# Linear attention on one core: norms of the queries split in token quarters, their factors multiplied in among the last queries, and all low halves on VectorE

## The chip, the cores and the metric

The kernel runs on one core of one Trainium2 chip. The metric is the device time of one execution in microseconds (us); for a kernel it is the median of several runs.

## The reference, cut to what matters

The program is two transformer layers over x of shape (4, 512, 256). The change lies in the first block alone, linear attention with 16 query heads and 4 key/value heads of 128, followed by a residual and a layer norm:

```
q = x @ Wq.T + bq ; k = x @ Wk.T + bk ; v = x @ Wv.T + bv     # 16, 4, 4 heads of 128
sq, sk = elu(q) + 1, elu(k) + 1
kv    = einsum('bhsd,bhse->bhde', sk, v)                       # k, v repeated for 4 query heads
norm  = einsum('bhsd,bhd->bhs', sq, sk.sum(axis=2))
attn  = (sq @ kv) / (norm[..., None] + 1e-6)
x     = layernorm(x + concat_heads(attn) @ Wo.T)
```

The 3 blocks behind it (a gated low-rank update, softmax attention, experts) make up the second phase.

## The kernel before, in words

The engines run queues of their own, in program order, and wait on semaphores. Phase 1 is `layer0_attention`, phase 2 `update_attention_experts`. Phase 1 handles the 4 batches of 512 tokens one after the other; what follows is one batch. P is 128, T is 512. "Head n" is the n-th in `ORDER0`: head j of each of the 4 groups g, then j + 1.

1. Keys and values: TensorE, L274, 4 token tiles, 48 matmuls of 512 columns. Every product of this phase with weights is done in three passes (`split_passes`) with values split into a high and a low half of type fp32r.
2. Queries: `query(n)` on TensorE (L303) is six matmuls of 512 columns into one of three PSUM banks `bank_q`. ScalarE takes min and exp (L426, L428), VectorE makes `sq[n]` (L522). `query(n)` waits until VectorE has read the bank of `query(n-3)`.
3. Norms: `norm(j)` (L316) multiplies the `sq` of the four heads of one j by `ksel` (the key sums placed in columns), 4 matmuls of 512 columns, each in its own 32 rows of `bank_n`. Two j share a half. VectorE then adds an epsilon (`invert`, L538), takes the reciprocal in two pieces of 256 columns (`invert_tokens`, L544), ScalarE makes a high half (`factor_hi`, L419), VectorE the rest (`parts`, L549).
4. Maps: `output_map(p)` (L331) makes kv @ Wo for two heads; ScalarE and VectorE split it (`map_hi` L414, `map_lo` L527). There are 8 maps per batch, in 4 buffers.
5. Factors: `factor(n)` (L345) is one matmul of 512 columns that spreads the reciprocal norms of head n over 128 rows of a `bank_q` bank. VectorE multiplies it into `sq[n]` (L601, "scale"). ScalarE makes `s_hi` (L468). The low half `s_lo` is VectorE's for even n (`scaled_lo`, L533) and GpSimd's for odd n (L229). `s_hi` and `s_lo` have two buffers each, so `s_hi(n)` waits for `project(n-2)`.
6. Projections: `project(n)` (L361) is 12 matmuls of 256 columns (4 token tiles, 3 passes) that add up in `bank_y`; it waits for `s_hi(n)` and `s_lo(n)`.

TensorE's order for a batch is written out by hand: keys and values, queries 0 to 2, the kv state (L286) and the key sums (L290), queries 3 to 15 with maps 0 to 3 behind queries 4, 6, 14 and 15 and norms 0 to 2 behind queries 5, 9 and 13, then factor 0, factor 1, norm 3, and for n = 0 to 15: `factor(n+2)`, `project(n)`, with maps 4 to 7 behind projects 1, 3, 5 and 7. VectorE's order in the last part is, for each n: scale(n), and for odd n `scaled_lo(n-1)` behind it; the inversion of the second half stands behind scales 0 to 2, a `map_lo` behind scales 4, 6, 8 and 10, the split of the next batch's x (`split_x`, 1024 columns) behind scale 12.

Of the kernel before, what the change touches and what calls it, by code (L numbers as in the profile page):

```python
# [16 lines left out]
P = 128  # L17
# [9 lines left out]
ORDER0 = [(g, j) for j in range(J0) for g in range(G0)]  # L27

# [85 lines left out]
def layer0_attention(nc, a, kept):  # L114

    with ExitStack() as ctx:
# [18 lines left out]
        pick_raw, pick = sb("pick_raw", [H0]), sb("pick", [H0], F32R)  # L135
# [7 lines left out]
        ksel = sb("ksel", [G0, J0, 32])  # L143
# [3 lines left out]
        den, rn = sb("den", [T]), sb("rn", [T])  # L147
        rn_c, rn_parts = sb("rn_c", [T], F32R), sb("rn_parts", [2, T], F32R)
        m_hi, m_lo = sb("m_hi", [4, 2 * D], F32R), sb("m_lo", [4, 2 * D], F32R)
        s_hi, s_lo = sb("s_hi", [2, T], F32R), sb("s_lo", [2, T], F32R)  # L150
# [25 lines left out]
        s_lo_ready = [sem("s_lo_ready_even"), sem("s_lo_ready_odd")]  # L176
# [5 lines left out]
        PARTS_AT = 10  # L182
        MAP_AT = (4, 6, 14, 15)
# [10 lines left out]
        def _(sp):  # L194
# [12 lines left out]
            with sp.Fori(0, B - 1) as b:  # L207
                after = sp.snap(b + 1)
                sp.wait_ge(xT_hi_ready, after)
                sp.wait_ge(xT_lo_ready, after)  # L210
                sp.dma_start(xT[:, :, :], a["xT"][:, bass.ds(after, 1)].rearrange("p o k n -> p (o k) n")).then_inc(xT_in, 16)
# [9 lines left out]
        def _(pool):  # L221
# [3 lines left out]
            def scaled_lo(b, n):  # L225

                pool.wait_ge(s_hi_ready, H0 * b + n + 1)
                at_least(pool, s_lo_ready[1], H0 // 2 * b + n // 2)
                pool.tensor_tensor(s_lo[:, 1, :], sq[:, n, :], s_hi[:, 1, :].bitcast(F32), ALU.subtract).then_inc(s_lo_ready[1], 1)  # L229

            def keep(b):

                pool.wait_ge(res_ready, b + 1)
                pool.wait_ge(s_lo_ready[1], H0 // 2 * (b + 1))
                pool.tensor_copy(tiles(xs, b), res[:, :, :]).then_inc(res_kept, 1)
# [9 lines left out]
            def body(b, last):  # L245
                sum_keys(b)
                if last:
                    keep(b - 1)
                pool.wait_ge(sk_sum_step, (NT - 1) * (b + 1))
                for n in range(1, H0, 2):  # L250
                    if n == 1:
                        at_least(pool, res_kept, b)
                    scaled_lo(b, n)
# [7 lines left out]
        def _(pe):  # L261
# [30 lines left out]

            def query(b, n):
                g, j = ORDER0[n]
                hd = slice((J0 * g + j) * DH0, (J0 * g + j + 1) * DH0)
                if n < 3:
                    at_least(pe, scaled, H0 * b)
                else:
                    pe.wait_ge(sq_ready, H0 * b + n - 2)
                i = 0  # L300
                for k in range(KD):
                    for lhs, rhs in split_passes(wq_hi[:, k, hd], wq_lo[:, k, hd], xT_hi[:, k, :], xT_lo[:, k, :]):
                        mm = pe.matmul(bank_q[n % 3][:, :], lhs, rhs, start=i == 0, stop=i == 3 * KD - 1)  # L303
                        i += 1
                mm.then_inc(q_done, 1)

            def norm(b, j):
# [27 lines left out]
            def factor(b, n):  # L335
# [5 lines left out]
                if n < 3:  # L341
                    pe.wait_ge(sq_ready, H0 * b + H0 + n - 2)
                else:
                    pe.wait_ge(scaled, H0 * b + n - 2)
                pe.matmul(bank_q[(H0 + n) % 3][:, :], pick[:, h:h + 1].broadcast_to([P, P]), rn_parts[:, n // (H0 // 2), :],  # L345
                          start=True, stop=True).then_inc(bc_done, 1)

            def project(b, n):
# [3 lines left out]
                pe.wait_ge(s_lo_ready[n % 2], H0 // 2 * b + n // 2 + 1)  # L352
# [4 lines left out]
                for t in range(NT):  # L357
                    tok = slice(t * P, (t + 1) * P)
                    for i, (lhs, rhs) in enumerate(split_passes(s_hi[:, n % 2, tok], s_lo[:, n % 2, tok], m_hi[:, m, cols], m_lo[:, m, cols])):
# [9 lines left out]
            def body(b, first):  # L369
                pe.wait_ge(xT_hi_ready, b + 1)  # L370
                pe.wait_ge(xT_lo_ready, b + 1)
# [11 lines left out]
                for n in range(3, H0):  # L383
# [21 lines left out]
        def _(act):  # L405
            def split_x(b):
                act.wait_ge(xT_in, 16 * (b + 1))
                at_least(act, q_done, H0 * b)
                act.activation(xT_hi[:, :, :], xT[:, :, :], ACT.Copy).then_inc(xT_hi_ready, 1)
# [6 lines left out]
            def factor_hi(b, half_):  # L416
                act.wait_ge(rn_ready, 2 * (2 * b + half_ + 1))
# [3 lines left out]
            def query_exp(b, n):  # L421
# [4 lines left out]
                act.activation(eq[:, n % 3, :], bank_q[n % 3][:, :], ACT.Relu, bias=bq_neg[:, h:h + 1], scale=-1.0).then_inc(eq_capped, 1)  # L426
# [14 lines left out]
            def body(b, first, more):  # L441
# [15 lines left out]
                for n in range(3, H0):  # L457
                    query_exp(b, n)
                    if n in MAP_AT:
                        map_hi(b, MAP_AT.index(n))  # L460
                    if n == PARTS_AT + 3:
                        factor_hi(b, 0)
                for n in range(H0):
                    if n == 4:
                        factor_hi(b, 1)
                    act.wait_ge(scaled, H0 * b + n + 1)
                    at_least(act, y_done, H0 * b + max(0, n - 1))
                    act.activation(s_hi[:, n % 2, :], sq[:, n, :], ACT.Copy).then_inc(s_hi_ready, 1)  # L468
                    if n in (3, 5, 7, 9):
                        map_hi(b, 4 + (n - 3) // 2)  # L470
                    if n == 10 and more:
                        split_x(b + 1)

            split_weights(0)
            split_x(0)
# [6 lines left out]
        def _(dve):  # L482
            def split_x(b):
                dve.wait_ge(xT_hi_ready, b + 1)
                at_least(dve, q_done, H0 * b)
                dve.tensor_tensor(xT_lo[:, :, :], xT[:, :, :], xT_hi[:, :, :].bitcast(F32), ALU.subtract).then_inc(xT_lo_ready, 1)
# [30 lines left out]
            def query(b, n):  # L517
# [4 lines left out]
                dve.scalar_tensor_tensor(out=sq[:, n, :], in0=bank_q[n % 3][:, :], scalar=bq1[:, h:h + 1], in1=eq[:, n % 3, :],  # L522
# [6 lines left out]
            def scaled_lo(b, n):  # L529
# [3 lines left out]
                dve.tensor_tensor(s_lo[:, 0, :], sq[:, n, :], s_hi[:, 0, :].bitcast(F32), ALU.subtract).then_inc(s_lo_ready[0], 1)  # L533

            def invert(b, half_):

                dve.wait_ge(norm_done, 2 * b + half_ + 1)
                dve.tensor_scalar(den[:, :], bank_n[:, :], DEN_EPS, None, ALU.add).then_inc(den_ready, 1)  # L538

            def invert_tokens(b, half_, i):  # L540

                dve.wait_ge(den_ready, 2 * b + half_ + 1)
                tok = slice(i * T // 2, (i + 1) * T // 2)
                dve.reciprocal(rn[:, tok], den[:, tok]).then_inc(rn_ready, 1)  # L544
# [14 lines left out]
            def residual_stats(b):  # L559

                dve.wait_ge(res_ready, b + 1)
                for t in range(NT):
                    dve.bn_stats(bn[:, t, :], res[:, t, :]).then_inc(bn_ready, 1)
                dve.wait_ge(bn_ready, NT * (b + 1))
# [3 lines left out]
            def body(b, last, more):  # L568
# [6 lines left out]
                for i in range(2):  # L575
                    at_least(dve, s_lo_ready[i], H0 // 2 * b)
# [1278 lines left out]
```

## Time and profile before

| what | value |
|---|---|
| runs timed | 834.54, 835.08, 848.41 us; median 835.08 |
| profiled execution | 842.74 us |
| its span (first to last instruction) | 840.7 us |
| TensorE, weight loads | 723.7 us (86%), 486.0 us (58%) |
| VectorE, ScalarE, GpSimd | 528.6 (63%), 410.0 (49%), 106.4 (13%) |
| mean granted TensorE clock | 0.9 |

Phase 1 takes the first 361 us of the span or so, phase 2 the rest. In the profile PE is TensorE's matmuls, PEld its weight loads, DVE VectorE, ACT ScalarE, POOL GpSimd. The duration of a matmul includes its pipeline, so a chain of matmuls is read by the distance of their starts.

### The profile page before, as it was taken

The page shows a single profiled execution, that of the slowest core. Times are in us where ns is not written, and L with a number is a line of the kernel's source. Part 1 is how long each engine was busy: PE and PEld are TensorE (multiplying, and loading weights), DVE is VectorE, ACT ScalarE, POOL GpSimd, SP SyncE. Part 2 cuts the span into 40 slices and gives each one's busy share as a digit, 9 for nine tenths or more (in the row PEclk, how much of TensorE's full clock was granted, in tenths as well). Part 3 has the DMA queues.
Part 4 walks back from the last instruction along what each step waited for, and adds up shares of the span by engine and source line. Part 5 has one row for each costly group of instructions (what it writes and reads, how often), then busy time and mean ns, then how long its engine had stood idle before and what let it go on. Part 6 is the DMA issues. An engine that isn't in the chain of part 4 may idle for free.

```text
span 840.7 us, 10896 instructions
## 1 busy us (share of the span) xinstructions
PE 723.7 (86%) x3836; PEld 486.0 (58%) x3836; DVE 528.6 (63%) x1135; ACT 410.0 (49%) x742; POOL 106.4 (13%) x102
## 2 busy tenths in 40 slices
PE   4798999889989998934678998899999999999764
PEld 3667886778768776833433453355555545455454
DVE  3568556855586558553365777777978787762243
ACT  3474347434754465421202674576556665556422
POOL 0301320132013301315000100010002000000000
PEclk9999999999999999975755896899999999879968
DMA  9200000010000100010650182028100840000000
GB/s 350 76 1 0 27 0 1 1 40 0 0 0 0 69 0 0 0 47 1 75 75 2 23 102 29 2 38 95 23 2 17 93 70 2 1 2 27 26 0 26
DMA packets 13588, 28.22 MB, mean 34 GB/s; under 512 B 2593, under 2 KB 3433, under 8 KB 13033
## 3 DMA queue, kind: packets, MB, share of 16 engines
q1 hardware_dynamic: 13544, 27.67, 17.6%
q8 instruction: 24, 0.39, 0.2%
q14 instruction: 20, 0.16, 0.1%
HBM read 12.59 MB, written 2.10 MB: 17 GB/s over the span
## 4 chain that ended last, share of the span: by engine, by line
PE 39%; DVE 10%; ACT 3%; issue 2%; DMA 2%; POOL 1%; SPq 0%; ACTq 0%; POOLq 0%; DVEq 0%
PE bank_st L1012 8%; PE bank_c L1025 6%; DVE nmax L1512 5%; PE side L962 4%; PE side L1083 3%; PE bank_s L993 3%; PE side L1114 2%; PE side L1043 2%; PE side L945 1%; DMA ks<-qk_lo 1%; PE side L914 1%; PE side L976 1%; ACT xk L1249 1%; DVE ln_bn L1470 1%; PE bank_t L1033 1%
## 5 line engine op out<-in xcount | busy, mean ns | idle before, releaser
L1512 DVE TENSOR_REDUCE nmax<-bank_s 128x1 f32<-128x512 f32 x256 | 164.8, 685 | 75.6 <-PE bank_s L993 74.8
L1293 ACT ACTIVATE shared<-bank_st 128x512 f32<-128x512 f32 x256 | 139.1, 596 | 78.2 <-PE bank_st L1012 77.4
L993 PE MATMUL bank_s<-ks,qs 48*128 48x512 f32 x256 | 117.6, 526 | 19.4 <-DVE nmax L1512 11.6
L1012 PE MATMUL bank_st<-qs,ks 50*128 50x512 f32 x256 | 106.2, 487 | 8.3 <-ACT shared L1293 4.7
L361 PE MATMUL bank_y<-m_hi,s_lo 128*128 128x256 f32 x256 | 75.4, 294 | 16.4 <-ACT s_hi L468 8.4
L522 DVE SCALAR_TENSOR_TENSOR sq<-bank_q,bq,eq 128x512 f32<-128x512 f32 x64 | 46.6, 738 | 51.3 <-ACT eq L428 51.3
L468 ACT ACTIVATE s_hi<-sq 128x512 fp32r<-128x512 f32 x64 | 40.4, 631 | 78.8 <-PE bank_y L361 66.1
L1025 PE MATMUL bank_c<-shared,v 128*32 128x512 f32 x512 | 76.9, 676 | 0.9 <-ACT shared L1293 0.9
L1012 PEld LDWEIGHTS bank_st<-qs,ks 50*128 50x128 f32 x256 | 43.2, 201 | 57.3 <-issue 32.1
L361 PE MATMUL bank_y<-m_lo,s_hi 128*128 128x256 f32 x256 | 73.9, 288 | 0.0
L361 PE MATMUL bank_y<-m_hi,s_hi 128*128 128x256 f32 x256 | 73.7, 288 | 0.0
L229 POOL TENSOR_TENSOR s_lo<-sq,s_hi 128x512 fp32r<-128x512 f32 x32 | 43.4, 1355 | 225.2 <-ACT s_hi L468 225.2
L993 PEld LDWEIGHTS bank_s<-ks,qs 48*128 48x128 f32 x256 | 47.5, 209 | 38.9 <-DVE nmax L1512 29.7
L601 DVE TENSOR_TENSOR sq<-sq,bank_q 128x512 f32<-128x512 f32 x64 | 43.4, 679 | 32.5 <-PE bank_q L345 32.5
L361 PEld LDWEIGHTS bank_y<-m_hi,s_lo 128*128 128x128 f32 x256 | 50.3, 197 | 21.8 <-issue 13.0
L426 ACT ACTIVATE eq<-bank_q,bq_neg 128x512 f32<-128x512 f32 x64 | 44.1, 689 | 35.1 <-PE bank_q L303 33.4
L303 PE MATMUL bank_q<-xT_hi,wq_lo 128*128 128x512 f32 x128 | 54.7, 427 | 0.0
L361 PEld LDWEIGHTS bank_y<-m_lo,s_hi 128*128 128x128 f32 x256 | 50.4, 197 | 1.7
L303 PE MATMUL bank_q<-xT_lo,wq_hi 128*128 128x512 f32 x128 | 50.6, 396 | 0.0
L303 PE MATMUL bank_q<-xT_hi,wq_hi 128*128 128x512 f32 x128 | 50.6, 395 | 0.0
L846 POOL TENSOR_TENSOR ln_rstd<-ln_var,half 128x4 f32<-128x4 f32 x12 | 12.1, 1012 | 303.7 <-DVE ln_var L111 303.7
L361 PEld LDWEIGHTS bank_y<-m_hi,s_hi 128*128 128x128 f32 x256 | 50.4, 197 | 0.0
(242 smaller groups left out, 1353.2 us busy)
## 6 DMA issues: line engine op xcount, KB each, us to landing
qs<-qk_hi SPq DMA_DIRECT2D x16, 256.0 KB, 5.5
ks<-qk_hi SPq DMA_DIRECT2D x16, 256.0 KB, 10.0
xT<-in_xT SPq DMA_DIRECT2D x4, 512.0 KB, 5.1
sq<-in_wqT SPq DMA_DIRECT2D x2, 1024.0 KB, 9.0
wo<-in_woT SPq DMA_DIRECT2D x1, 2048.0 KB, 12.6
xs<-in_x SPq DMA_DIRECT2D x1, 2048.0 KB, 17.5
qs<-qk_lo SPq DMA_DIRECT2D x8, 256.0 KB, 7.8
ks<-qk_lo SPq DMA_DIRECT2D x8, 256.0 KB, 10.5
```

Source lines behind the costliest of these rows:

```text
L229: pool.tensor_tensor(s_lo[:, 1, :], sq[:, n, :], s_hi[:, 1, :].bitcast(F32), ALU.subtract).then_inc(s_lo_ready[1], 1)
L303: mm = pe.matmul(bank_q[n % 3][:, :], lhs, rhs, start=i == 0, stop=i == 3 * KD - 1)
L361: mm = pe.matmul(bank_y4[:, t, :], lhs, rhs, start=n == 0 and i == 0 and t % 2 == 0, stop=n == H0 - 1 and i == 2, skip_group_check=True)
L426: act.activation(eq[:, n % 3, :], bank_q[n % 3][:, :], ACT.Relu, bias=bq_neg[:, h:h + 1], scale=-1.0).then_inc(eq_capped, 1)
L468: act.activation(s_hi[:, n % 2, :], sq[:, n, :], ACT.Copy).then_inc(s_hi_ready, 1)
L522: dve.scalar_tensor_tensor(out=sq[:, n, :], in0=bank_q[n % 3][:, :], scalar=bq1[:, h:h + 1], in1=eq[:, n % 3, :], op0=ALU.add, op1=ALU.max ...
L601: dve.tensor_tensor(sq[:, n, :], sq[:, n, :], bank_q[(H0 + n) % 3][:, :], ALU.mult).then_inc(scaled, 1)
L993: pe.matmul(bank_s[u % 2][:, :], qs[part, b % 2, slot, t * P:(t + 1) * P], ks[part, b % 2, slot, :], start=True, stop=True).then_inc(s_don ...
L1012: pe.matmul(bank_st[u % 2][:, :], ks[part, b % 2, slot, kt * P:(kt + 1) * P], qs[part, b % 2, slot, :], start=True, stop=True).then_inc(st ...
L1025: mm = pe.matmul(bank_c[32 * j:32 * j + 32, :], v[:, b % 2, kt, 4 * g + j, :], probs[:, (4 * s + j) % SLOTS, :], start=kt == 0, stop=kt == 3)
L1293: act.activation(probs[:, u % SLOTS, :], bank_st[u % 2][:, :], ACT.Exp, scale=SCALE1).then_inc(p_ready, 1)
L1512: dve.tensor_reduce(nmax[:, g, t, j:j + 1], bank_s[u % 2][:, :], AX.X, ALU.max, negate=True).then_inc(max_ready, 1)
```

## The change

All of it is in phase 1. A "quarter" is 128 tokens.

- Norms: each of the 4 quarters gets rows of its own, so a norm is 16 matmuls of 128 columns in place of 4 of 512, and the norms of a half fill 128 columns of `bank_n` in place of 512. `den`, `rn`, `rn_c`, `rn_parts` shrink from 512 to 128 columns; the reciprocal is one instruction per half.
- Factors: a factor is 4 matmuls of 128 columns, each with weights of its own (`pick` has 64 columns), in place of one of 512.
- Orders: maps 0 to 3 stand behind queries 4, 6, 8, 10, norms 0 and 1 behind queries 6 and 9. Factors 0 to 3 and projects 0 to 2 are placed among queries 13 to 15 and norms 2 and 3. From n = 3 on TensorE runs `factor(n+1)`, `project(n)` in place of `factor(n+2)`, `project(n)`. A table `USES` gives the `bank_q` bank of each use in this order.
- Low halves: `s_hi` and `s_lo` have three buffers, and VectorE makes all 16 low halves. GpSimd keeps the key sums and the copy of the residual.
- `split_x` runs in two pieces of 512 columns; the statistics of the last residual are spread over queries 3, 5 and 7.

```diff
+USES = ([("query", n) for n in range(13)] + [("factor", 0), ("query", 13), ("factor", 1), ("query", 14), ("factor", 2), ("query", 15)]
+        + [("factor", n) for n in range(3, H0)])
...
-        s_hi, s_lo = sb("s_hi", [2, T], F32R), sb("s_lo", [2, T], F32R)
+        s_hi, s_lo = sb("s_hi", [3, T], F32R), sb("s_lo", [3, T], F32R)
...
-        PARTS_AT = 10
-        MAP_AT = (4, 6, 14, 15)
+        MAP_AT = (4, 6, 8, 10)
...
+            def q_bank_free(b, kind, n):
+
+                k = USE[kind, n]
+                if k < 3:
+                    at_least(pe, scaled, H0 * b)
+                elif USES[k - 3][0] == "query":
+                    pe.wait_ge(sq_ready, H0 * b + USES[k - 3][1] + 1)
+                else:
+                    pe.wait_ge(scaled, H0 * b + USES[k - 3][1] + 1)
...
-                for g in range(G0):
-                    mm = pe.matmul(bank_n[32 * g:32 * g + 32, :], ksel[:, g, j, :], sq[:, G0 * j + g, :],
-                                   start=j % 2 == 0, stop=j % 2 == 1)
+                for q in range(QUARTERS):
+                    tok = slice(q * P, (q + 1) * P)
+                    for g in range(G0):
+                        mm = pe.matmul(bank_n[32 * g:32 * g + 32, (j // 2) * P:(j // 2 + 1) * P], ksel[:, g, QUARTERS * (j % 2) + q, :],
+                                       sq[:, G0 * j + g, tok], start=j % 2 == 0 and q == 0, stop=j % 2 == 1 and q == QUARTERS - 1)
...
+                q_bank_free(b, "factor", n)
+                for q in range(QUARTERS):
+                    mm = pe.matmul(q_bank("factor", n)[:, q * P:(q + 1) * P], pick[:, QUARTERS * h + q:QUARTERS * h + q + 1].broadcast_to([P, P]),
+                                   rn_parts[:, n // (H0 // 2), :], start=True, stop=True)
+                mm.then_inc(bc_done, 1)
...
-                for n in range(3, H0):
+                for n in range(3, 13):
                     query(b, n)
                     if n in MAP_AT:
                         output_map(b, MAP_AT.index(n))
-                    if n % G0 == 1 and n > G0:
-                        norm(b, n // G0 - 1)
+                    if n in (6, 9):
+                        norm(b, n // 3 - 2)
                 pe.wait_ge(setup_done, 4)
                 factor(b, 0)
+                query(b, 13)
+                norm(b, 2)
                 factor(b, 1)
-                norm(b, J0 - 1)
-                for n in range(H0):
-                    if n + 2 < H0:
-                        factor(b, n + 2)
+                query(b, 14)
+                project(b, 0)
+                factor(b, 2)
+                query(b, 15)
+                project(b, 1)
+                factor(b, 3)
+                project(b, 2)
+                norm(b, 3)
+                for n in range(3, H0):
+                    if n + 1 < H0:
+                        factor(b, n + 1)
                     project(b, n)
-                    if n % 2 == 1 and n < 8:
-                        output_map(b, 4 + n // 2)
+                    if n in (3, 5, 7, 9):
+                        output_map(b, 4 + (n - 3) // 2)
...
+            def scaled_hi(b, n):
+                act.wait_ge(scaled, H0 * b + n + 1)
+                at_least(act, y_done, H0 * b + max(0, n - 2))
+                act.activation(s_hi[:, n % 3, :], sq[:, n, :], ACT.Copy).then_inc(s_hi_ready, 1)
...
+                scale(b, 0)
+                query(b, 12)
+                scaled_lo(b, 0)
+                scale(b, 1)
+                query(b, 13)
+                scaled_lo(b, 1)
+                query(b, 14)
+                scale(b, 2)
+                scaled_lo(b, 2)
+                query(b, 15)
+                scale(b, 3)
+                scale(b, 4)
+                scaled_lo(b, 3)
+                invert(b, 1)
+                scaled_lo(b, 4)
+                for n in range(5, H0):
+                    scale(b, n)
                     if n == 5:
                         parts(b, 1)
-                    if n in (4, 6, 8, 10):
-                        map_lo(b, 4 + (n - 4) // 2)
-                    if n == 12 and more:
-                        split_x(b + 1)
+                    if n > 5:
+                        scaled_lo(b, n - 1)
+                    if n in (6, 8, 10, 12):
+                        map_lo(b, 4 + (n - 6) // 2)
+                    if n in (9, 11) and more:
+                        split_x(b + 1, (n - 9) // 2)
+                scaled_lo(b, H0 - 1)
```

ScalarE's order: `factor_hi(0)` behind query 10, `scaled_hi` of heads 0 to 2 behind queries 12 to 14, then `scaled_hi(n)` for n = 3 to 15 with `factor_hi(1)` behind head 4.

## Rows read from the trace of the kernel before

The columns of a windows row are: the stretch, its length in us, busy us of PE, PEld, DVE, ACT and POOL with the number of instructions, the granted TensorE clock (1.00 is 2.4 GHz, 0.50 is 1.2 GHz), DMA share, GB/s.

**Rows 1.** The page: busy us of the engines, share of the span, instructions.
```profile
PE 723.7 (86%) x3836; PEld 486.0 (58%) x3836; DVE 528.6 (63%) x1135; ACT 410.0 (49%) x742; POOL 106.4 (13%) x102
```
**Rows 2.** Windows, batch 1 (columns below): queries 3 to 15; turn; projections.
```profile
124.80:151.20 26.40, 25.52 (x119) 17.73 (x119) 17.09 (x36) 18.77 (x31) 0.00 (x0) 1.00 0.00 1
151.20:155.90 4.70, 2.26 (x12) 0.64 (x12) 4.45 (x8) 2.36 (x4) 0.09 (x1) 1.00 0.01 2
155.90:190.70 34.80, 31.66 (x222) 29.95 (x223) 21.23 (x29) 12.79 (x20) 11.27 (x8) 0.95 0.09 25
```
**Rows 3.** Windows: query 3 to last projection, first batch, and sum over 4.
```profile
40.50:104.40 63.90, 59.11 (x351) 48.21 (x350) 42.87 (x64) 35.60 (x57) 10.32 (x8) 0.97 0.03 9
...
sum 259.10, PE 235.99 PEld 191.66 DVE 169.62 ACT 136.32 POOL 43.35; mean PE 59.00 PEld 47.91 DVE 42.40 ACT 34.08 POOL 10.84
```
**Rows 4.** Timeline of PE, batch 1 (start, us, what, [idle before <-releaser]).
```profile
124.76 0.48 PE L303 MATMUL bank_q<-xT_hi,wq_lo 128*128 128x512 f32 x1
...
129.99 1.06 PE L316 MATMUL bank_n<-sq,ksel 128*32 128x512 f32 x8
...
141.66 0.40 PE L303 MATMUL bank_q<-xT_hi,wq_lo 128*128 128x512 f32 x1
143.06 0.40 PE L303 MATMUL bank_q<-xT_hi,wq_lo 128*128 128x512 f32 x1
...
155.93 0.36 PE L361 MATMUL bank_y<-m_hi,s_lo 128*128 128x256 f32 x1 [1.78 <-ACT s_hi L468]
...
189.16 0.36 PE L361 MATMUL bank_y<-m_hi,s_lo 128*128 128x256 f32 x1 [0.87 <-POOL s_lo L229]
190.67 0.40 PE L274 MATMUL bank_a<-wkv,xT_lo 128*128 128x512 f32 x1
```
**Rows 5.** Timeline of PE, batch 1: two projections, a factor, a map between.
```profile
167.56 0.28 PE L361 MATMUL bank_y<-m_hi,s_lo 128*128 128x256 f32 x1
...
171.51 0.40 PE L345 MATMUL bank_q<-rn_parts,pick 128*128 128x512 f32 x1
171.74 0.28 PE L361 MATMUL bank_y<-m_hi,s_lo 128*128 128x256 f32 x1
...
173.17 1.03 PE L331 MATMUL bank_a<-wo,kvT 128*128 128x256 f32 x4
173.84 0.58 PE L345 MATMUL bank_q<-rn_parts,pick 128*128 128x512 f32 x1
174.26 0.28 PE L361 MATMUL bank_y<-m_hi,s_lo 128*128 128x256 f32 x1
```
**Rows 6.** Timelines of DVE and POOL, batch 1: scale, low halves, reciprocal.
```profile
143.13 1.75 DVE L544 RECIPROCAL rn<-den 128x256 f32<-128x256 f32 x1
...
154.39 0.68 DVE L601 TENSOR_TENSOR sq<-sq,bank_q 128x512 f32<-128x512 f32 x1
154.99 0.68 DVE L533 TENSOR_TENSOR s_lo<-sq,s_hi 128x512 fp32r<-128x512 f32 x1
...
171.94 0.69 DVE L601 TENSOR_TENSOR sq<-sq,bank_q 128x512 f32<-128x512 f32 x1 [0.38 <-PE bank_q L345]
187.74 1.28 POOL L229 TENSOR_TENSOR s_lo<-sq,s_hi 128x512 fp32r<-128x512 f32 x1 [2.69 <-ACT s_hi L468]
```
**Rows 7.** Timeline of PE, batch 1: 128-column and 1-column matmuls, own weights.
```profile
120.38 3.73 PE L286 MATMUL bank_a<-sk,v 128*128 128x128 f32 x32
123.95 0.95 PE L290 MATMUL bank_a<-ones,sk_sum 128*128 128x1 f32 x8
```
**Rows 8.** Windows of 4 us in four places of the span.
```profile
152.00:156.00 4.00, 1.57 (x10) 0.44 (x10) 4.00 (x7) 1.56 (x3) 0.18 (x1) 1.00 0.01 2
156.00:160.00 4.00, 4.00 (x20) 3.90 (x21) 4.00 (x5) 0.63 (x1) 1.09 (x1) 0.57 0.02 4
240.00:244.00 4.00, 2.22 (x9) 1.93 (x10) 4.00 (x6) 1.26 (x2) 1.29 (x1) 0.71 0.00 0
788.00:792.00 4.00, 2.02 (x14) 0.45 (x10) 1.32 (x8) 2.51 (x6) 1.21 (x2) 1.00 0.00 0
```

More of the change, by code:

```diff
@@ L208, in _ @@
                 after = sp.snap(b + 1)
-                sp.wait_ge(xT_hi_ready, after)
-                sp.wait_ge(xT_lo_ready, after)
+                halves = sp.snap(KD * after)
+                sp.wait_ge(xT_hi_ready, halves)
+                sp.wait_ge(xT_lo_ready, halves)
                 sp.dma_start(xT[:, :, :], a["xT"][:, bass.ds(after, 1)].rearrange("p o k n -> p (o k) n")).then_inc(xT_in, 16)
@@ L248, in body @@
                     keep(b - 1)
[L249 to L253, printed above, removed]
             body(0, False)
@@ L295, in query @@
                 hd = slice((J0 * g + j) * DH0, (J0 * g + j + 1) * DH0)
[L296 to L299, printed above, removed]
+                q_bank_free(b, "query", n)
                 i = 0
@@ L302, in query @@
                     for lhs, rhs in split_passes(wq_hi[:, k, hd], wq_lo[:, k, hd], xT_hi[:, k, :], xT_lo[:, k, :]):
-                        mm = pe.matmul(bank_q[n % 3][:, :], lhs, rhs, start=i == 0, stop=i == 3 * KD - 1)
+                        mm = pe.matmul(q_bank("query", n)[:, :], lhs, rhs, start=i == 0, stop=i == 3 * KD - 1)
                         i += 1
@@ L358, in project @@
                     tok = slice(t * P, (t + 1) * P)
-                    for i, (lhs, rhs) in enumerate(split_passes(s_hi[:, n % 2, tok], s_lo[:, n % 2, tok], m_hi[:, m, cols], m_lo[:, m, cols])):
+                    for i, (lhs, rhs) in enumerate(split_passes(s_hi[:, n % 3, tok], s_lo[:, n % 3, tok], m_hi[:, m, cols], m_lo[:, m, cols])):
                         mm = pe.matmul(bank_y4[:, t, :], lhs, rhs,
@@ L458, in body @@
                     query_exp(b, n)
+                    if n == 10:
+                        factor_hi(b, 0)
                     if n in MAP_AT:
                         map_hi(b, MAP_AT.index(n))
-                    if n == PARTS_AT + 3:
-                        factor_hi(b, 0)
-                for n in range(H0):
+                    if n in (12, 13, 14):
+                        scaled_hi(b, n - 12)
+                for n in range(3, H0):
+                    scaled_hi(b, n)
                     if n == 4:
                         factor_hi(b, 1)
[L466 to L471, printed above, removed]
-                        split_x(b + 1)
+                    if n in (5, 7, 9, 11):
+                        map_hi(b, 4 + (n - 5) // 2)
+                    if n in (8, 10) and more:
+                        split_x(b + 1, (n - 8) // 2)
             split_weights(0)
-            split_x(0)
+            for k in range(KD):
+                split_x(0, k)
             body(0, True, True)
@@ L574, in body @@
                 at_least(dve, s_hi_ready, H0 * b)
-                for i in range(2):
-                    at_least(dve, s_lo_ready[i], H0 // 2 * b)
+                at_least(dve, s_lo_ready, H0 * b)
                 for n in range(3):
@@ L584, in body @@
                     for r in range(2):
-                        cp = dve.tensor_copy(dst[:, 4 * r:4 * r + 3 * 33 + 1:33], bank_a[1][:, g:g + 1].broadcast_to([P, J0]))
+                        cp = dve.tensor_copy(dst[:, 16 * r:16 * r + 7 * 33 + 1:33], bank_a[1][:, g:g + 1].broadcast_to([P, 2 * QUARTERS]))
                 cp.then_inc(ksel_ready, 1)
-                for n in range(3, H0):
+                for n in range(3, 12):
                     query(b, n)
+                    if n in (3, 5) and last:
+                        residual_stats(b - 1, (0, 1) if n == 3 else (2, 3))
                     if n == 7 and last:
-                        residual_stats(b - 1)
-                    if n == PARTS_AT:
+                        residual_merge(b - 1)
+                    if n == 9:
                         invert(b, 0)
-                    if n in (PARTS_AT, PARTS_AT + 1):
-                        invert_tokens(b, 0, n - PARTS_AT)
-                    if n == PARTS_AT + 4:
+                    if n == 10:
                         parts(b, 0)
@@ L622, in _ @@
             residual(B - 1)
-            residual_stats(B - 1)
+            residual_stats(B - 1, range(NT))
+            residual_merge(B - 1)
 def by_tile(x):
```

85 lines of the change are left out of this document (37 added, 48 removed).

## The prediction

> **What bounds the kernel now.** I read the page first: TensorE is the busiest engine at 86% of the span and VectorE has 63% [rows 1]. The change touches phase 1 alone, so the next view is the windows by stage. In batch 1 TensorE is busy 25.5 of 26.4 us through queries 3 to 15, 2.3 of 4.7 us in the turn to the projections, and 31.7 of 34.8 us in the projections [rows 2]. Phase 1 is TensorE's, and its idle time lies at the turn and behind GpSimd's low halves. The reader should see both in the timeline: project 0 starts 1.78 us late for ScalarE's high half, project 15 starts 0.87 us late for GpSimd's low half [rows 4]. The same stretch, query 3 to last projection, takes 259 us in the four batches, 64.8 us each, with TensorE busy 59 [rows 3]. So at most some 6 us a batch can be won by taking waits away. Two per cent of this kernel are 16.7 us, about what a measurement of it can tell from no change.
>
> **The prices, from rows.** A query is 1.40 us (141.66 to 143.06) [rows 4]. A project is 12 matmuls, 1.43 us from its start to that of the next map (171.74 to 173.17); a factor of one matmul costs 0.23 (171.51 to 171.74); a map 0.67 and the first matmul behind it 0.2 to 0.3 more [rows 5]. On VectorE a scale takes 0.60 us to the start of the next instruction and a low half ends 0.68 after its start; a scale starts some 0.03 us after the factor's matmul ends (171.51 + 0.40, 171.94) [rows 5, 6]. From the end of a low half to the first matmul that uses it 0.14 us pass (187.74 + 1.28, 189.16), and that matmul is followed 0.07 us later than the rest [rows 4, 6].
>
> **The steady part, projects 5 to 15.** This decides. TensorE's new order is factor(n+1), project(n); VectorE's is scale(n+1), `scaled_lo(n)`. `project(5)` needs low half 5, which VectorE starts behind scale 6; scale 6 needs factor 6, and factor 6 stands on TensorE behind `project(4)`. So each link waits for the last: project(n-1), factor(n+1), scale(n+1), low half n, project(n). Nothing of it lies beside other work. Before, factor(n+2) was issued a project earlier, and the two engines ran beside each other. The third buffer of `s_hi` and `s_lo` does not help, as what is late is the scale in front, not the buffer. What queues behind the waiting scale on VectorE is the low half that TensorE needs; what queues behind the waiting project on TensorE is the next factor.
>
> One round: project 1.43; the new factor's four matmuls, the fourth starts 3 spacings later and ends 0.22 after that. The spacing is not shown for these weights and this type; the nearest rows are 32 records of 128 columns in 3.57 us and 8 records of a single column in 0.81, each with 128 columns of weights: 0.11 in both [rows 7]. A lower end is half the present 256-column spacing of 0.12, 0.06. I take 0.11: 0.33 + 0.22 = 0.55. Then 0.04 to VectorE, scale 0.60, low half 0.68, 0.14 + 0.07 back to TensorE. The sum is 3.5 us. With a map behind the project it is 0.85 more, 4.35. Project 5 to 14 is 9 rounds, three with a map (behind 5, 7, 9): 6 x 3.5 + 3 x 4.35 = 34.05. Project 15 follows 14 without a stall, since its own low half comes directly behind the one before it: 2 x 1.43. Together 36.9 us. Now it is 23.1 (167.56 to 190.67) [rows 4, 5]: **+13.8 us a batch**. The `map_lo`, `split_x` and `parts` of this stretch fall into the 1.9 us in which VectorE waits for project and factor, and cost nothing while the chain stands.
>
> The Trainium skill, "TensorE: Matmul & The Clock Gate", section "Back-to-back issue gap", puts a sustained stream of load and matmul pairs at 128 columns at about 81 ns each, where the rows above show 0.11 us. By that page a factor would be 0.09 us shorter, and 13 of them in each of 4 batches would take 5 us off the sum (an estimate from the page); I go by the rows.
>
> **Queries 3 to 11.** New: 9 queries x 1.40 = 12.6, four maps x 0.95 = 3.8 (two moved here), two norms. A norm now takes 1.06 us, 1.0 without the end of its pipeline, for 8 records of 512 columns, and they overlap by fours [rows 4]. As 32 records of 128 columns it moves as many columns; at the lower end it stays 1.0, at the upper end, with no overlap, it is 32 x 0.11 = 3.6 [rows 7]. The rows of the four groups are untouched, so I stay near the lower end: 1.2, and 0.1 for the query behind it. Sum 12.6 + 3.8 + 2.6 = 19.0 us against 16.9 now (124.76 to 141.66): **+2.1**.
>
> **Query 12 to project 5.** Walked with the prices above, in us from query 12: factor 0 at 1.4; query 13 waits for `sq[11]` until 2.4; norm 2 3.9 to 5.1; factor 1, query 14 5.5; project 0 at 7.0; factor 2 8.4; query 15 8.9; project 1 10.3; factor 3, project 2 12.1; norm 3 13.6 to 14.8; factor 4, whose result comes at 15.4. Scale 4 stands in front of low half 3, so project 3 starts only at 16.9. Map 4, factor 5, project 4 at 19.6; factor 6 at 21.0, scale 6, low half 5, and project 5 at 23.2. Now the same takes 25.9 (141.66 to 167.56) [rows 4, 5]. The saving is real: projects 0 to 2 fill the turn, and the reciprocals, 2 x 1.75 us for a half now [rows 6], shrink to one of some 0.9 us. **-2.7**, though the two maps are gone from here.
>
> **Other edits at nothing.** Smaller `den`, `rn_c` and `parts` lie in VectorE's and ScalarE's waits. Eight low halves more are 8 x 0.60 = 4.8 us on VectorE, against some 5.2 saved on reciprocals (2 x 2 x 1.75 to 2 x 0.9): by itself no bound, with 42 of 65 us busy [rows 3]. The split statistics and `split_x` pieces are the same columns. The DMA of the next xT waits for both halves, as before, and lands long before it is needed. If this cover fails it costs under 1 us a batch.
>
> **Sum.** 19.0 + 23.2 + 36.9 = 79.1 us a batch, against 64.8: +14.3, for four batches +57. The profiled execution is 842.7 us (span 840.7), which gives 900; the median of the runs shown is 7.7 us lower, and 835.1 + 57 = **892 us**.
>
> **Rivals.**
> *The clock falls as well.* TensorE would idle some 1.5 us in every 3.5. Rows cut both ways: with TensorE busy 1.6 of 4 us the clock went to 0.57 in the next window, with 2.2 of 4 it stood at 0.71, with 2.0 of 4 it stayed at 1.00 [rows 8]. At 1.2 GHz a project takes 12 x 0.21 = 2.6 us, so a plain round is longer by 1.1 and, with the factor and the maps, the batch by some 16. In all batches that is 956 us, in half of them 924. The maps and the dense stages between speak against all. The same page of the Trainium skill, Part 1, says that the clock is throttled by default and released by activity, which is this rival.
> *Norms without overlap.* 3.6 in place of 1.2 us, four a batch: +38, 930 us. Against it: the groups keep their rows.
> *The chain is looser than I read it (the other side).* The place is factor(n+1) in the steady part. If its result reached VectorE while project(n-1) still ran, the chain would not bind, and only TensorE's own work would be left: 13 queries 18.2, 8 maps 7.4, 4 norms 4.8, 16 factors 7.2, 16 projects 22.9, together 60.5 a batch, 4.3 less than now, 818 us. It decides where a round falls below the present mean of 2.16 us ((189.16 - 167.56) / 10), that is, if 1.3 of the 3.5 us overlapped. The program order on both queues speaks against it.
> *Half a chain.* Hand-overs and factors cheaper than priced, or most rounds hiding the scale: half of the 13.8 gone in each batch, 865 us.
>
> **How the numbers follow.** The chain at full clock 0.70, with a lower clock 0.14, norms without overlap 0.06, half a chain 0.06, loose 0.04. The main case by itself runs from 876 (factor at 0.06 a matmul, norm 1.0, hand-overs 0.1 shorter: 4 us a batch) to 905. The range for 8 in 10 is 870 to 932. Faster by over 2%: 0.02; within 2%: 0.03; slower by over 2%: 0.95.
>
> **What would show it.** In the profile after, between projects 5 and 14, the timeline of PE should show a wait of some 1.5 us before each project, released by the low half of VectorE; each low half starts 0.60 us after a scale, and each scale waits for the factor. Starts of projects 3.5 and 4.35 us apart. GpSimd has no low half. A stretch from query 3 to last project of 79 us, and project 0 some 7 us behind query 12. Wrong would be: projects under 2.5 us apart, a clock of 0.5 in most of the stretch, or norms over 2 us.

## The result, and the profile after

| | before | after |
| --- | --- | --- |
| median of the runs (4 each, taken together) | 840.5 us | 899.9 us (895.3 to 903.1) |
| ratio after / before | | 1.073, 95% interval 1.061 to 1.085 |
| profiled execution, and its span | 842.7 us, 840.7 us | 903.1 us, 901.3 us |

The change makes the kernel 7.3% slower. The ratio leaves out the run before of 848.4 us as a slow one; the two medians alone would give 1.071. The forecast was 892 us from the median and 900 us from the profiled execution, in a range of 870 to 932.

The page after, its row of engines and the groups of phase 1 that changed most (busy us, mean ns of one, then idle time just before them and what ended it):

```profile
PE 740.6 (82%) x4412; PEld 517.6 (57%) x4412; DVE 523.5 (58%) x1163; ACT 405.3 (45%) x746; POOL 63.4 (7%) x70
...
L366 PE MATMUL bank_y<-m_hi,s_lo 128*128 128x256 f32 x256 | 77.1, 301 | 64.8 <-ACT s_hi L447 64.8
...
L447 ACT ACTIVATE s_hi<-sq 128x512 fp32r<-128x512 f32 x64 | 40.4, 631 | 146.3 <-DVE sq L559 146.2
L559 DVE TENSOR_TENSOR sq<-sq,bank_q 128x512 f32<-128x512 f32 x64 | 43.9, 686 | 105.6 <-PE bank_q L349 105.6
```

TensorE has 17 us more to do than before [rows 1], and all engines are idle for a larger share of a longer span. TensorE waits 64.8 us at the projections, and VectorE 105.6 us at the scales for TensorE's factors: these two waits are the ends of one ring. ScalarE waits for VectorE's scales; as is shown below, it stands beside the ring.

The windows from query 3 to the last projection, now of all four batches (length, busy us of PE, PEld, DVE, ACT, POOL, granted clock, DMA share, GB/s):

```profile
41.60:121.50 79.90, 63.48 (x493) 55.87 (x493) 41.15 (x71) 34.51 (x58) 0.00 (x0) 0.98 0.03 8
142.10:221.10 79.00, 62.30 (x497) 54.76 (x497) 41.55 (x78) 32.83 (x55) 0.00 (x0) 1.00 0.04 11
241.40:320.40 79.00, 62.29 (x496) 54.75 (x496) 41.55 (x78) 32.87 (x55) 0.00 (x0) 1.00 0.00 0
340.80:423.00 82.20, 65.50 (x496) 57.45 (x495) 40.38 (x76) 31.71 (x52) 0.00 (x0) 0.96 0.00 0
sum 320.10, PE 253.57 PEld 222.83 DVE 164.63 ACT 131.92 POOL 0.00; mean PE 63.39 PEld 55.71 DVE 41.16 ACT 32.98 POOL 0.00
```

320.1 us against 259.1 [rows 3]: 61.0 us, about what the span grew (60.6). A batch takes 80.0 us in the mean, where 79.1 was forecast. TensorE's busy time in it rises by 4.4 us; the other 10.9 are waits. The clock stays at 0.96 to 1.00.

The turn of batch 2 in the timeline of PE (start, us, what, [idle before <-releaser]): query 12, query 13, norm 2, factor 1, project 0, norm 3, project 3, project 5.

```profile
259.98 0.40 PE L307 MATMUL bank_q<-xT_hi,wq_lo 128*128 128x512 f32 x1
...
262.37 0.50 PE L307 MATMUL bank_q<-xT_hi,wq_lo 128*128 128x512 f32 x1 [0.44 <-DVE sq L542]
...
263.96 1.08 PE L322 MATMUL bank_n<-sq,ksel 128*32 128x128 f32 x32
264.97 0.66 PE L349 MATMUL bank_q<-rn_parts,pick 128*128 128x128 f32 x4
...
266.91 0.28 PE L366 MATMUL bank_y<-m_hi,s_lo 128*128 128x256 f32 x1
...
273.57 1.08 PE L322 MATMUL bank_n<-sq,ksel 128*32 128x128 f32 x32
...
276.72 0.36 PE L366 MATMUL bank_y<-m_hi,s_lo 128*128 128x256 f32 x1 [1.48 <-ACT s_hi L447]
...
283.00 0.35 PE L366 MATMUL bank_y<-m_hi,s_lo 128*128 128x256 f32 x1 [1.47 <-ACT s_hi L447]
```

The turn itself did get better: project 0 runs 6.9 us behind query 12, and the wait of 1.78 us in front of it [rows 4] is gone. It takes 23.0 us from query 12 to project 5, against 25.9.

One round of the steady part, from the timeline of all engines (project 6 is at 287.35, project 7 at 290.88):

```profile
285.96 0.69 DVE L559 TENSOR_TENSOR sq<-sq,bank_q 128x512 f32<-128x512 f32 x1 [2.51 <-PE bank_q L349]
286.56 0.69 DVE L553 TENSOR_TENSOR s_lo<-sq,s_hi 128x512 fp32r<-128x512 f32 x1
286.68 0.63 ACT L447 ACTIVATE s_hi<-sq 128x512 fp32r<-128x512 f32 x1 [3.77 <-DVE sq L559]
...
287.35 0.35 PE L366 MATMUL bank_y<-m_hi,s_lo 128*128 128x256 f32 x1 [1.43 <-ACT s_hi L447]
...
288.85 0.56 PE L349 MATMUL bank_q<-rn_parts,pick 128*128 128x128 f32 x4
...
289.45 0.69 DVE L559 TENSOR_TENSOR sq<-sq,bank_q 128x512 f32<-128x512 f32 x1 [2.20 <-PE bank_q L349]
290.05 0.68 DVE L553 TENSOR_TENSOR s_lo<-sq,s_hi 128x512 fp32r<-128x512 f32 x1
290.17 0.63 ACT L447 ACTIVATE s_hi<-sq 128x512 fp32r<-128x512 f32 x1 [2.38 <-DVE sq L559]
...
290.88 0.35 PE L366 MATMUL bank_y<-m_hi,s_lo 128*128 128x256 f32 x1 [1.47 <-ACT s_hi L447]
```

Follow it once around. Project 6 starts at 287.35; the factor behind it at 288.85 and ends at 289.41; the scale starts at 289.45; the low half behind it ends at 290.73; project 7 starts at 290.88. That is 3.53 us for 1.43 us of projection, and at each moment one engine works for the ring. One name in it misleads. The profile puts TensorE's wait down to ScalarE's `s_hi`, which ends at 290.80. But that high half starts after the scale of head 8 and belongs to head 8; project 7 needs the high half of head 7, which started at 286.68 and was ready at 287.31. What it needs and has just got is the low half that ended at 290.73. Experiment e4 tests this.

### The profile page after: what moved, and what is told of

Read it like the earlier page. It is cut to its first block, busy times and chain, and to the rows that moved or that the text cites. A ratio compares the mean times of both kernels' runs of the same rounds, so it can differ in the third digit from the quotient of the medians.

```text
span 901.3 us, 12085 instructions
## 1 busy us (share of the span) xinstructions
PE 740.6 (82%) x4412; PEld 517.6 (57%) x4412; DVE 523.5 (58%) x1163; ACT 405.3 (45%) x746; POOL 63.4 (7%) x70
## 4 chain that ended last, share of the span: by engine, by line
PE 36%; DVE 9%; ACT 3%; issue 2%; DMA 2%; POOL 1%; SPq 0%; ACTq 0%; POOLq 0%; DVEq 0%
PE bank_st L1049 8%; PE bank_c L1062 6%; DVE nmax L1549 4%; PE side L1120 4%; PE side L999 3%; PE bank_s L1030 2%; PE side L1151 2%; PE side L982 1%; DMA ks<-qk_lo 1%; PE side L1080 1%; PE side L951 1%; PE side L1013 1%; ACT xk L1286 1%; DVE ln_bn L1507 1%; PE bank_t L1070 1%
## 5 line engine op out<-in xcount | busy, mean ns | idle before, releaser
L366 PE MATMUL bank_y<-m_hi,s_lo 128*128 128x256 f32 x256 | 77.1, 301 | 64.8 <-ACT s_hi L447 64.8
L559 DVE TENSOR_TENSOR sq<-sq,bank_q 128x512 f32<-128x512 f32 x64 | 43.9, 686 | 105.6 <-PE bank_q L349 105.6
L307 PE MATMUL bank_q<-xT_lo,wq_hi 128*128 128x512 f32 x128 | 50.5, 394 | 0.0
L307 PE MATMUL bank_q<-xT_hi,wq_hi 128*128 128x512 f32 x128 | 50.5, 394 | 0.0
L553 DVE TENSOR_TENSOR s_lo<-sq,s_hi 128x512 fp32r<-128x512 f32 x64 | 43.7, 682 | 3.3 <-ACT s_hi L447 2.8
L271 PE MATMUL bank_a<-wkv,xT_hi 128*128 128x512 f32 x128 | 41.5, 405 | 0.0
```

The source lines that it names most:

```text
L271: mm = pe.matmul(bank[:, :], lhs, rhs, start=n == 0, stop=n == 3 * KD - 1)
L307: mm = pe.matmul(q_bank("query", n)[:, :], lhs, rhs, start=i == 0, stop=i == 3 * KD - 1)
L366: mm = pe.matmul(bank_y4[:, t, :], lhs, rhs, start=n == 0 and i == 0 and t % 2 == 0, stop=n == H0 - 1 and i == 2, skip_group_check=True)
L553: dve.tensor_tensor(s_lo[:, n % 3, :], sq[:, n, :], s_hi[:, n % 3, :].bitcast(F32), ALU.subtract).then_inc(s_lo_ready, 1)
L559: dve.tensor_tensor(sq[:, n, :], sq[:, n, :], q_bank("factor", n)[:, :], ALU.mult).then_inc(scaled, 1)
```

## Experiments

The theory: the price is the ring project(n-1), factor(n+1), scale(n+1), low half n, project(n), which the order of the factors on TensorE closes. Its rivals: VectorE is too full with all the low halves; the quarters cost TensorE time; or the clock explains it. The kernel before, timed again beside them, had medians of 834.7 to 843.6 us; a ratio is to those runs.

All these kernels have the phase 2 of before, and yet from its first matmul to the end it takes 466 to 477 us in their profiles (474 before, 472 after). What an edit does to phase 1 is therefore given beside the total as the time at which that matmul starts: 366.7 us before, 429.0 after.

**e1_lead_two: open the ring on TensorE's side.** The kernel after, with factors two projects ahead again.

```diff
                 norm(b, 3)
+                factor(b, 4)
                 for n in range(3, H0):
-                    if n + 1 < H0:
-                        factor(b, n + 1)
+                    if n + 2 < H0:
+                        factor(b, n + 2)
                     project(b, n)
```

> The changed kernel with one edit: factor 4 is issued behind norm 3, and from n = 3 on TensorE runs factor(n+2), project(n) again; all else stays (quarters, three buffers, VectorE's order, all low halves there). Theory (the factor one project ahead closes a chain over TensorE and VectorE): the chain opens, because scale(n+1) can run while project(n-1) does. A round is then TensorE's own 1.43 + 0.45 = 1.9 us in place of 3.53, 2.7 with a map in place of 4.35; query 3 to last project about 62 to 64 us a batch in place of 79.5; time 830 to 845. Rival (the loss lies in the 128-column matmuls, in VectorE's eight more low halves, or in the clock, not in the order): hardly any gain, 880 or more.

Measured: 825.9 us, 0.984 of before (0.974 to 0.993). Phase 2 starts at 356.2 us. One factor's place is worth 74 us, and without that loss the rest of the change is a gain. TensorE in batch 1 now runs from project to project in 1.87 us, or 2.75 with a map, with no wait between:

```profile
169.94 0.33 PE L366 MATMUL bank_y<-m_hi,s_lo 128*128 128x256 f32 x1
...
171.81 0.33 PE L366 MATMUL bank_y<-m_hi,s_lo 128*128 128x256 f32 x1
...
174.56 0.33 PE L366 MATMUL bank_y<-m_hi,s_lo 128*128 128x256 f32 x1
...
176.43 0.33 PE L366 MATMUL bank_y<-m_hi,s_lo 128*128 128x256 f32 x1
```

The same VectorE with the same 16 low halves a batch keeps up, so it was never the bound. The wait at the first matmuls of the projections fell from 64.8 us to:

```profile
L366 PE MATMUL bank_y<-m_hi,s_lo 128*128 128x256 f32 x256 | 75.2, 294 | 4.4 <-ACT s_hi L448 4.1
```

**e2_low_first: open it on VectorE's side.** The factor stays one ahead, but low half n-1 goes in front of scale n.

```diff
                 for n in range(5, H0):
+                    if n > 5:
+                        scaled_lo(b, n - 1)
                     scale(b, n)
...
-                    if n > 5:
-                        scaled_lo(b, n - 1)
```

> The changed kernel with one edit on VectorE: in the loop over n = 5 to 15 low half n-1 stands ahead of scale n, not behind it. TensorE's order stays. Theory: low half n no longer waits for factor n+1, so a chain goes over two rounds: factor(n) behind project(n-2), 0.55 + 0.04, scale 0.68, high half 0.63 + 0.03, low half 0.68, 0.2, and project 1.43 make 4.3 us for two rounds, 2.15 each; a batch 66 to 68 us, time 845 to 860. It would gain less than issuing the factor two ahead, since the high half comes into the chain. Rival (VectorE has too much work, whatever its order): no gain, about 900.

Measured: 850.7 us, 1.012 (1.003 to 1.020). Phase 2 starts at 374.1 us. In the timeline of batch 1 two rounds, of which one has a map, take 5.19 us, and two behind the last map 4.33, where 4.3 was expected. The wait in front of every other projection shrinks to 0.16 to 0.43 us, and now names VectorE's low half; the 1.48 us before project 3 are still there:

```profile
L366 PE MATMUL bank_y<-m_hi,s_lo 128*128 128x256 f32 x256 | 76.3, 298 | 15.5 <-DVE s_lo L553 8.9 <-ACT s_hi L447 5.9 <-issue 0.2
```

Cutting the ring at a second link frees most of it too (49 us); what is left is that a factor one project ahead gives VectorE just too little time.

**e3_pad_behind and e4_pad_between: the same instruction off and on the ring.** Both add ten additions of 128x512 a batch into a buffer that nobody reads at that time; e3 puts each behind the low half, e4 between scale and low half.

```diff
+            def pad(b, n):
+                at_least(dve, pad_done, 10 * b + n - 6)
+                dve.tensor_tensor(zk[:, 1, :], bk[:, :], bv[:, :], ALU.add).then_inc(pad_done, 1)
...
                     if n > 5:
+                        pad(b, n)
                         scaled_lo(b, n - 1)
```

> The changed kernel with one more VectorE instruction of 128 x 512 (an addition of two constants into a buffer that is idle then) in each of the 10 steps n = 6 to 15, BEHIND low half n-1. Theory (serial chain, in which VectorE has slack behind the low half): no effect, each stretch from query 3 to the last project within 0.5 us of 79.5, as in the changed kernel. Rival (VectorE is the bound): 10 x 0.6 = 6 us a batch, +24 us.

Measured: 893.0 us, one run; the period of a batch is 99.37 us, after's is 99.35. Forty more VectorE instructions off the ring cost nothing (the median of after is 899.9).

> The same additional instruction, BETWEEN scale n and low half n-1. Theory: it lies on the chain and each round grows by 0.6 us, from 3.53 to 4.15; +6 us a batch, stretches of 85.5, +24 to +26 us in all. Rival (TensorE waits for ScalarE's high half, as the rows of the waits name it, since the high half of the next head follows the scale and not the low half): no effect, as the added instruction does not delay the high half.

Measured: 974.9 us, one run: 75 us more where some 25 were expected. The wait in front of a projection grew from 1.47 to 2.08 us, by the 0.61 us that the ring asks for. Phase 2 starts at 496.5 us, 67 later than in after: 24 of them are the forty instructions, and the other 43 go with TensorE's clock. Its busy time rose from 740.6 to 788.9 us for the same 4412 records. In the timeline of batch 2 a project after such a wait starts like this:

```profile
341.41 0.55 PE L367 MATMUL bank_y<-m_hi,s_lo 128*128 128x256 f32 x1 [2.08 <-DVE s_lo L554]
341.76 0.42 PE L367 MATMUL bank_y<-m_lo,s_hi 128*128 128x256 f32 x1
341.98 0.42 PE L367 MATMUL bank_y<-m_hi,s_hi 128*128 128x256 f32 x1
...
344.12 1.91 PE L338 MATMUL bank_a<-wo,kvT 128*128 128x256 f32 x4
345.46 1.31 PE L350 MATMUL bank_q<-rn_parts,pick 128*128 128x128 f32 x4
...
348.80 0.36 PE L367 MATMUL bank_y<-m_hi,s_lo 128*128 128x256 f32 x1 [2.03 <-ACT s_hi L448]
```

Spacings of 0.21 us in place of 0.12, and a project of 2.7 us: the lower of the two clocks, 1.2 GHz. The window 300 to 400 us has a granted clock of 0.81, where the same window of after has 0.98:

```profile
300.00:400.00 100.00, 77.39 (x441) 69.66 (x441) 46.72 (x81) 28.34 (x48) 5.16 (x4) 0.81 0.04 15
```

So the rival "the clock falls as well", which came true in after for three short spells only, stood 0.6 us of wait away from it (by this one run). And the releaser is settled:

```profile
L367 PE MATMUL bank_y<-m_hi,s_lo 128*128 128x256 f32 x256 | 90.6, 354 | 88.9 <-DVE s_lo L554 54.5 <-ACT s_hi L448 34.3
```

An instruction between scale and low half cannot delay the high half, and yet the wait grew by all of its length; more than half of it now carries the low half's name.

**e5_low_on_vector: the low halves alone.** The kernel before with three buffers and all low halves on VectorE.

```diff
-        s_hi, s_lo = sb("s_hi", [2, T], F32R), sb("s_lo", [2, T], F32R)
+        s_hi, s_lo = sb("s_hi", [3, T], F32R), sb("s_lo", [3, T], F32R)
...
-                    if n % 2 == 1:
+                    if n > 0:
                         scaled_lo(b, n - 1)
...
+                scaled_lo(b, H0 - 1)
```

> The kernel before with one part of the change alone: three buffers for the high and low halves, and all low halves on VectorE (low half n-1 behind every scale n); TensorE's order, with the factor two ahead, and the whole norms and factors stay. Theory (moving the low halves is a gain by itself, and hurts only behind a factor that is one ahead): TensorE's waits for GpSimd's low halves (7.6 us in all) and most of those at the end of each batch go, 826 to 832 against the kernel before, 8 to 12 us less. Rival (VectorE's extra 4.8 us a batch are what costs): slower than before by 5 us or more.

Measured: 839.1 us, 1.002 (0.998 to 1.006): no gain that can be measured, and the expectation was missed. In the profile GpSimd's waits are gone, and the first matmul of phase 2 comes at 361.53 us against 366.65 before: 5 us in phase 1, some 1.3 a batch. The two waits of 1.78 and 0.80 us before projects 0 and 1 are still there, and they are the larger part of what was to be had. Why even the 5 us do not show in the medians stays open: phase 2 varies by more than that, and the ten runs had granted clocks of 0.892 to 0.897, those of before 0.892 to 0.915.

**e6_quarters_alone: the quarters alone.** The kernel before with the norms, factors and reciprocals in quarters, nothing moved.

```diff
-                for g in range(G0):
-                    mm = pe.matmul(bank_n[32 * g:32 * g + 32, :], ksel[:, g, j, :], sq[:, G0 * j + g, :],
+                for q in range(QUARTERS):
+                    tok = slice(q * P, (q + 1) * P)
+                    for g in range(G0):
+                        mm = pe.matmul(bank_n[32 * g:32 * g + 32, (j // 2) * P:(j // 2 + 1) * P], ksel[:, g, QUARTERS * (j % 2) + q, :],
+                                       sq[:, G0 * j + g, tok], start=j % 2 == 0 and q == 0, stop=j % 2 == 1 and q == QUARTERS - 1)
```

> The kernel before with another part alone: quarters in own rows for norms and factors; orders, GpSimd's odd low halves and two buffers stay. Theory: a factor costs TensorE 0.21 us more (0.45 against 0.23), some 13 times a batch where it has no idle time, +2.7 us; norms cost nothing more; the shorter reciprocals give back 1.5 to 2.5 us at the turn. Together 0 to +5 us against the kernel before. Rival (the quarters carry the loss of the change): +20 us or more.

Measured: 839.5 us, 1.001 (0.996 to 1.005). Phase 2 starts at 365.3 us, 1.3 earlier than before. Two effects cancel: TensorE's busy time rose from 723.7 to 732.5 us, and its waits at the first matmuls of the projections fell from 16.4 to 8.5.

**e7_best_quarters: what is left to win.** e1, and low half 3 in front of scale 4.

```diff
                 scale(b, 3)
-                scale(b, 4)
                 scaled_lo(b, 3)
+                scale(b, 4)
                 invert(b, 1)
```

> The changed kernel with the factor two ahead, as in e1_lead_two, and on VectorE low half 3 ahead of scale 4. Theory: project 3, which waited 1.02 us there for low half 3 behind scale 4, starts as soon as norm 3 and factors 4 and 5 are issued; 1 us a batch, 4 us less than e1_lead_two: 822. Rival (project 3 is late for something else): the same as e1_lead_two.

Measured: 823.8 us, 0.985 (0.976 to 0.994). The wait of 1.02 us before project 3 that e1 still had is gone, and in all of phase 1 the projections wait 0.3 us:

```profile
L366 PE MATMUL bank_y<-m_hi,s_lo 128*128 128x256 f32 x256 | 75.1, 293 | 0.3
```

It beats both kernels. By medians it is not told apart from e1, but phase 2 starts at 352.5 us, 3.7 earlier than in e1, where 4 was expected. Against before phase 1 is 14 us shorter (10 in e1); the other 7 or 8 us by which these two profiles are shorter lie in phase 2, whose code is the same, so I do not count them as gain of the change.

**e8_whole_factors: the new order without the quarters.** e7 with norms and factors of 512 columns and each half's reciprocal in two pieces of 256, as before.

```diff
-                for q in range(QUARTERS):
-                    mm = pe.matmul(q_bank("factor", n)[:, q * P:(q + 1) * P], pick[:, QUARTERS * h + q:QUARTERS * h + q + 1].broadcast_to([P, P]),
-                                   rn_parts[:, n // (H0 // 2), :], start=True, stop=True)
-                mm.then_inc(bc_done, 1)
+                pe.matmul(q_bank("factor", n)[:, :], pick[:, h:h + 1].broadcast_to([P, P]), rn_parts[:, n // (H0 // 2), :],
+                          start=True, stop=True).then_inc(bc_done, 1)
...
                     scale(b, n)
-                    if n == 5:
+                    if n in (5, 6):
+                        invert_tokens(b, 1, n - 5)
+                    if n == 7:
                         parts(b, 1)
```

> e7_best_quarters with norms and factors whole again (512 columns; reciprocals in two pieces of 256 columns, the second half's behind scales 5 and 6). Theory: with the chain open TensorE is the bound, and each factor gives back 0.21 us, 16 x 0.21 x 4 = 13 us; VectorE's 3.5 us of reciprocals for a half lie beside it: 809 to 812. Rival (the reciprocals then stand in front of low halves 4 to 6 and cost 1.7 us each): 820 or more, no better than with quarters.

Measured: 847.1 us, 1.010 (1.002 to 1.019). The main expectation was wrong by 35 us. The timelines of DVE and PE in batch 1 show why:

```profile
165.56 1.74 DVE L566 RECIPROCAL rn<-den 128x256 f32<-128x256 f32 x1
167.23 0.63 DVE L555 TENSOR_TENSOR sq<-sq,bank_q 128x512 f32<-128x512 f32 x1
167.77 1.74 DVE L566 RECIPROCAL rn<-den 128x256 f32<-128x256 f32 x1
169.43 0.62 DVE L549 TENSOR_TENSOR s_lo<-sq,s_hi 128x512 fp32r<-128x512 f32 x1
```

```profile
149.12 0.79 PE L345 MATMUL bank_q<-rn_parts,pick 128*128 128x512 f32 x1 [2.52 <-DVE rn_parts L571]
...
170.20 0.55 PE L361 MATMUL bank_y<-m_hi,s_lo 128*128 128x256 f32 x1 [2.83 <-DVE s_lo L549]
```

Two reciprocals stand in front of a low half, and factor 0, now among the queries, comes before its parts are made. Behind each of the two waits the clock fell (project 5 takes 2.7 us in place of 1.4). The quarters cost nothing in the old order; with the reciprocals placed as here they are worth 23 us in the new one (847.1 against 823.8), 16 of them in phase 1 (368.9 against 352.5). Another place for the long reciprocals was not tried.

**e9_lead_one: the ring alone, in the kernel before.** e5, with the factors one project ahead.

```diff
-                    if n + 2 < H0:
-                        factor(b, n + 2)
+                    if 1 <= n < H0 - 1:
+                        factor(b, n + 1)
                     project(b, n)
```

> The kernel before with three buffers and all low halves on VectorE, and the factors one project ahead in place of two; norms, factors and reciprocals stay whole, and projects 0 to 2 stay behind the last norm. If the lead of one in the open chain alone sets the price, a plain round is project 1.43, factor 0.40 (one matmul from start to end), 0.04, scale 0.60, low half 0.68, hand-over and first matmul 0.21: 3.4 us, with a map 4.2, over projects 1 to 14 where the version with a lead of two takes some 2.2; that is some 15 us more in each of 4 batches, about 895 us (885 to 910). If the quarters or the new order of queries 12 to 15 are needed for the loss, it stays near 840.

Measured: 930.4 us, one run; phase 2 starts at 452.1 us. From the timeline of PE, plain rounds of 3.37 us and, with a map, 4.20:

```profile
188.13 0.36 PE L349 MATMUL bank_y<-m_hi,s_lo 128*128 128x256 f32 x1 [1.43 <-ACT s_hi L456]
...
191.50 0.35 PE L349 MATMUL bank_y<-m_hi,s_lo 128*128 128x256 f32 x1 [1.47 <-ACT s_hi L456]
...
195.70 0.36 PE L349 MATMUL bank_y<-m_hi,s_lo 128*128 128x256 f32 x1 [1.43 <-ACT s_hi L456]
199.07 0.36 PE L349 MATMUL bank_y<-m_hi,s_lo 128*128 128x256 f32 x1 [1.47 <-ACT s_hi L456]
```

The two rounds are as expected; the total is not, and that is my arithmetic. Ten rounds of 3.37 and four of 4.20 are 50.5 us, and with the last project and the slow start projects 0 to 15 take 55.0 us (179.26 to 234.29). In e5 they take 32.2 (155.62 to 187.85). That is 22.8 us a batch and 91 in all, where I had written 15 and 60. The ring alone, with no quarter and no moved query, costs more than the whole change, since it has 14 closed rounds where the change has 9.

## Why the prediction was right

**The steady part, +13.8 forecast.** Right. From project 5 to the end of batch 2 37.4 us pass (283.00 to 320.44), forecast 36.9, so +14.3. Plain rounds are 3.53 to 3.63 us and rounds with a map 4.35, forecast 3.5 and 4.35. The links by their rows: factor 0.56 (0.55), to VectorE 0.04 (0.04), scale 0.60, low half 0.68, to TensorE 0.15 (0.14), and 0.07 for the first matmul. That the loss is this ring, and not VectorE's load, is shown by e1, e2 and e3 against e4: two different cuts free it, a load off it costs nothing, one on it costs at once. e9 shows that it needs nothing else of the change.

**Queries 3 to 11, +2.1 forecast.** Right in sign, 0.5 us too high: 18.5 us, +1.6 (241.45 to 259.98) where 19.0 was forecast. The norm as 32 records takes 1.08 us, and 1.06 before [rows 4]; I had taken 1.2. "Norms without overlap" fell by that row.

**Query 12 to project 5, -2.7 forecast.** Right: 23.0 us against 23.2, -2.9. Project 3 waits 1.48 us behind scale 4, as the hand walk said; 1.02 of it is left in e1, and e7 removes that. The reciprocal takes 0.95 us for 128 columns, forecast some 0.9.

**The factor's price.** The spacing taken from rows was 0.11 us. Four matmuls in 0.56 us, of which the last takes 0.22 to its end, are 0.11 apart. The Trainium skill, "TensorE: Matmul & The Clock Gate", section "Back-to-back issue gap", gives some 81 ns for a sustained pair of weight load and matmul at 128 columns; this trace does not agree, and the sum by that figure would have been 5 us lower (an estimate from the Trainium skill's figure).

**Edits at nothing.** Right: e6 puts the quarters, with their dearer factors, at 0, e3 shows the slack on VectorE, and phase 2 is as it was (472 us from its first matmul to the end, 474 before).

**The sum.** Forecast +14.3 us a batch and +57; measured +15.2 and +61. That it came so close is in part luck. The three terms in bold compare with batch 1 of before (16.9 + 25.9 + 23.1 = 65.9 us) and add up to 13.2, while 14.3 was taken against the mean of the four batches (64.8); +13.2 a batch would have been +53. By the terms, batch 2 of after is indeed 13.1 above 65.9. What made up for the difference is that the first and the last batch grew by more, 16.0 and 18.4 us, and some 4.6 us of this are three spells at 1.2 GHz (76.79 to 84.62 and 376.10 to 384.01 where batch 2 takes 6.28 us, and 411.31 to 416.29 where it takes 3.6). The median came out 8 us above 892, of which 5.4 are the base: 840.5 in place of 835.1.

**The rivals.** "Looser chain" and "half a chain" fell by the rounds of 3.5 us. The clock stayed up in after's phase 1 but for those three spells, so its 0.14 went all but unused; e4 shows the mechanism real in this very stretch, with 43 of the 67 us by which its phase 1 grew. Part 1 of the Trainium skill's "TensorE: Matmul & The Clock Gate" has the clock throttled by default and released by activity; e4 agrees, with 0.81 to 0.86 from 100 to 400 us where after, with shorter waits, has 0.98 to 1.00.

Where my expectations failed: e1 (825.9 us, below the 830 to 845), e4 (the clock left out), e5 (the gain of a removed wait taken in full, while the waits of 1.78 and 0.80 us beside it stayed), e8 (a reciprocal of 1.74 us counted as covered, though a low half was queued behind it), e9 (a sum over too few rounds).

## What to carry to other kernels

When two engines pass work to each other, write one round as a ring across both program orders and count how many steps ahead each issues: with a lead of one in both, the round is the sum of all links (3.5 us here), with a lead of two the longer engine's own work (1.9 us). Moving the producer by one place was worth 74 us, far more than a third buffer or a better balance of the engines (e5, at most 5 us). And a change that loses may hold a gain: cut it in parts before dropping it. Once the ring was open the rest of this change gave 1.5% (e7; the interval is 0.6 to 2.4%), though the low halves alone (e5) and the quarters alone (e6) gave nothing that can be measured.

## What the runs showed of the hardware that I had not expected

- TensorE kept its full clock but for three short spells where it waited 1.43 to 1.57 us in front of each projection (after), and fell again and again to 1.2 GHz where it waited 2.03 to 2.17 us (e4, one run), so 24 us of VectorE work (40 instructions of 0.60) cost 75.
- A norm of 16 matmuls of 128 columns in four row ranges (32 records) takes 1.08 us, as much as one of 4 matmuls of 512 columns (8 records, 1.06), while 4 factor matmuls of 128 columns with weights for all 128 columns take 0.56 against 0.40 for one of 512.
- The name of a releaser can be that of a neighbour that ends 0.05 to 0.07 us later: `s_hi` was named for all 64.8 us of waits that belonged to the low half.
